# A kernel of attention, LSTM, three graph layers and a quantised product on one core: turned rows in the aggregation's bank, rounded passes in the first graph layer, products for the next scores behind the turned rows

## The reference, cut to what matters

```python
x = x + gat(layernorm(x), adj)        # 8 heads: masked softmax(q k / sqrt(32)) v, Wo, relu
x = x + lstm(layernorm(x))            # 256 steps over the nodes, 32 graphs at once
x = x + layers(layernorm(x), adj)     # below
x = x + fp8_product(layernorm(x))     # x and weight rounded to fp8, product, rescaled

def layers(x, adj):                   # L = 3
    for l in range(3):
        scores = (x @ w[l, :d])[:, :, None] + (x @ w[l, d:])[:, None, :] + b[l]
        scores = where(adj or own node, leaky(scores, 0.2), -inf)
        h = layernorm(x + softmax(scores) @ x) * g1[l] + beta1[l]
        ff = gelu(h @ W1[l] + b1[l]) @ W2[l] + b2[l]        # 256 -> 1024 -> 256
        x = layernorm(h + ff) * g2[l] + beta2[l]
    return x
```

## Time and profile before

| | us |
|---|---|
| median of 3 runs (2993.64 to 2996.24) | 2994.3 |
| profiled execution | 2992.49 |
| its span | 2990.7 |
| TensorE busy | 2683.2 (90%) |
| VectorE busy | 2052.4 (69%) |
| ScalarE busy | 1839.8 (62%) |
| GpSimd busy | 1620.6 (54%) |

### The profile page before, as it was taken

The page is one execution under the profiler, slowest core; times in us unless marked ns, Lnnn a source line. Parts: engine busy times, 40 slices in busy tenths (PEclk is TensorE's granted clock), DMA queues, the critical chain, the costliest instruction groups (busy, mean ns, idle before and its releaser), DMA issues. The chain is left out here.

```text
span 2990.7 us, 116485 instructions
## 1 busy us (share of the span) xinstructions
PE 2683.2 (90%) x44066; PEld 2435.4 (81%) x44224; DVE 2052.4 (69%) x6005; ACT 1839.8 (62%) x4930; POOL 1620.6 (54%) x2681
## 2 busy tenths in 40 slices
PE   6999999978888888859999999999999999999957
PEld 5777777767777777749999999899899999999956
DVE  6887888734444444446777776888888888888768
ACT  4666666644444444437777776777777677777734
POOL 6777777510000000037777765666666677788744
PEclk9999999989999999969999999999999999999979
DMA  3111111000000000020000011100000100000002
GB/s 92 40 35 35 35 41 38 13 10 13 12 13 12 13 13 13 13 76 25 26 23 25 26 44 31 27 7 9 9 7 9 45 9 9 9 7 9 8 25 91
DMA packets 110836, 74.59 MB, mean 25 GB/s; under 512 B 51504, under 2 KB 109360, under 8 KB 110512
## 3 DMA queue, kind: packets, MB, share of 16 engines
q1 hardware_dynamic: 96800, 61.03, 7.1%
q10 hardware_dynamic: 13968, 12.72, 1.4%
HBM read 51.68 MB, written 22.02 MB: 25 GB/s over the span
## 5 line engine op out<-in xcount | busy, mean ns | idle before, releaser
L1560 PE MATMUL g_H<-g_hT_upper,g_w_upper 128*128 128x256 f32 x1536 | 453.9, 295 | 0.0
L1560 PE MATMUL g_H<-g_hT_rest,g_w_upper 128*128 128x256 f32 x1536 | 436.0, 284 | 0.0
L1560 PE MATMUL g_H<-g_hT_upper,g_w_rest 128*128 128x256 f32 x1536 | 435.7, 284 | 0.0
L745 POOL COPY l_xt<-seq 128x64 f32 x256 | 60.6, 237 | 598.2 <-PE l_O L756 596.5
L1159 ACT ACTIVATE g_act_raw<-g_H,g_small 128x256 f32<-128x256 f32 x768 | 303.3, 469 | 22.2 <-PE g_H L1560 21.0
L329 ACT ACTIVATE a_probs<-a_S,a_nmax 128x256 f32<-128x256 f32 x512 | 236.7, 480 | 121.6 <-DVE a_nmax L422 88.9
L1051 POOL TENSOR_TENSOR g_h<-g_r,g_g_row 128x256 f32<-128x256 f32 x192 | 138.1, 741 | 294.7 <-DVE g_r L1360 294.0
L1560 PEld LDWEIGHTS g_H<-g_hT_rest,g_w_upper 128*128 128x128 f32 x1536 | 295.7, 193 | 2.5
L1560 PEld LDWEIGHTS g_H<-g_hT_upper,g_w_upper 128*128 128x128 f32 x1536 | 295.4, 192 | 2.7 <-DVE g_hT_rest L1308 0.2
L1587 PE MATMUL g_F<-g_w_upper,g_act_upper 128*128 128x256 f32 x1024 | 293.1, 286 | 4.5 <-DVE g_act_rest L1346 4.1
L1560 PEld LDWEIGHTS g_H<-g_hT_upper,g_w_rest 128*128 128x128 f32 x1536 | 295.8, 193 | 0.0
(11 more groups left out here) (222 smaller groups left out, 8658.8 us busy)
## 6 DMA issues: line engine op xcount, KB each, us to landing
gmask<-masks ACTq DMA_DIRECT2D x97, 128.0 KB, 2.0
x<-in_x_dram SPq DMA_DIRECT2D x32, 256.0 KB, 3.0
a_adj<-in_adj_dram SPq DMA_DIRECT2D x32, 256.0 KB, 2.7
hidden<-l_hs SPq DMA_DIRECT2D x512, 16.0 KB, 1.4
g_hs<-hidden SPq DMA_DIRECT2D x32, 256.0 KB, 2.7
out_dram<-q_res SPq DMA_DIRECT2D x32, 256.0 KB, 2.1
masks<-gmask SPq DMA_DIRECT2D x32, 128.0 KB, 1.7
g_w_raw<-in_L_gnn_W_dram SPq DMA_DIRECT2D x6, 512.0 KB, 4.0
```

The source lines that it names most:

```text
L745: pool.tensor_copy(xt[i][:, :, :], t.seq[:, :, s * 2 + i, :]).then_inc(xt_done, 1)
L1560: last = pe.matmul(hidden_bank[m // 2][:, m % 2 * N:(m % 2 + 1) * N], w[:, c, m * P:(m + 1) * P], x[:, c, :], start=(c == 0 and k == 0), s ...
```

## The change

Between attention and the end these parts are altered:

- graph layers: the rows are turned into `agg_bank`, the bias columns (`shift_bias`) into `turn_bank`; `turn_probs` no longer waits for `hT_done`, and a quarter of `up` goes ahead of it;
- first layer: `down` uses three rounded products for all banks but the first (`FIRST`), which stays float32 and goes between `aggregate` and the second half of `up`; `ON_ACT` gives ScalarE two of the roundings, and W2 is split there too;
- ScalarE: one bank's activations ahead of the slopes, `hT_out` between the dummy exponential and the exponentials; it makes the upper part of W1, which is split in halves;
- VectorE: `feed` ahead of `turned`, a bank's split between several steps, and `next_pair` behind `split_hT`;
- entry: LSTM outputs go by DMA into `t.nodes` directly, the first four with semaphores of their own; the start of the phase is reordered on all engines;
- attention: the first weights are waited for without Wo and biases; at the end `norm2` of the last two graphs is VectorE's, the one before the last is turned in `in_bank`, and weight scaling and bias split go ahead;
- last phase: its weight is loaded into `t.aw` during the third layer.

```diff
-                    sp.dma_start(w[:, :, :], src.rearrange("(c p) n -> p c n", p=P)).then_inc(weights_in, 16)
+                for w, src, done in ((wq, a["L0_gnn_Wq"], weights_in), (wk, a["L0_gnn_Wk"], weights_in),
+                                     (wv, a["L0_gnn_Wv"], weights_in), (wo, a["L0_gnn_Wo"], rows_in)):
...
+                split_bias()
                 spread_out(B - 1)
                 for b in range(B - 2, B):
                     rsqrt2(b)
-                    norm2(b)
-                split_bias()
...
+                    bank = in_bank if isinstance(b, int) and b == B - 2 else head_bank
+                    act.activation(t.seq[:, :, :, b], bank[:, :].rearrange("p (c n) -> p c n", c=KC),
...
-                rden_out(B - 1)
-                for b in range(B - 2, B):
-                    xn2T_out(b)
                 act.wait_ge(t.lstm_weights_in, LSTM_IN)
                 for w in (t.wx, t.wh):
                     act.activation(w[:, :, 0, :], w[:, :, 0, :], ACT.Copy, scale=0.5)
                     act.activation(w[:, :, 2:4, :], w[:, :, 2:4, :], ACT.Copy, scale=0.5)
+                rden_out(B - 1)
+                for b in range(B - 2, B):
+                    xn2T_out(b)
...
+                def norm2(b):
+
+                    dve.wait_ge(heads_ps, B)
+                    alone(dve, rstd2_done, b + 1, passed)
+                    for it in range(NT):
+                        last = dve.tensor_scalar(xn2[:, it, :], t.x[:, b, it, :], mv2[:, it, 0:1], rstd2[:, it, :],
+                                                 ALU.subtract, ALU.mult)
...
+                dve.wait_ge(weights_in, 3 * 16)
...
                 xnT_rest_out(0)
+                dve.wait_ge(rows_in, 5 * 16)
+                dve.memset(qscale[:, :], HD ** -0.5)
+                dve.tensor_scalar(bqs_col[:, :], bq_col[:, :], HD ** -0.5, None, ALU.mult).then_inc(bqs_done, 1)
+                moments1(1)
...
+                    if isinstance(b, int) and b == B - 2:
+                        pe.wait_ge(rden_done, B)
+                        turn(in_bank, xn2).then_inc(xn2T_ps, 1)
+                        return
...
+                    after(pe, xn2T_done, b if not isinstance(b, int) or b < B - 1 else B - 2)
...
+        ON_ACT = ((1, 3), (1, 3), (3,))
+        FIRST = (1, 0, 0)
...
+                def load_hidden(e, done):
+                    sp.dma_start(t.nodes[:, e, :, :], hidden[e].rearrange("(t p) d -> p t d", p=P)).then_inc(done, 16)
...
+                        load_hidden(4, hs_in)
+                        with sp.Fori(5, B) as e:
+                            sp.wait_ge(extra_x, e)
+                            load_hidden(e, hs_in)
+                sp.wait_ge(pair_done, 2 * (L - 1) * B)
+                sp.dma_start(t.aw[:, :, :], a["L1_ffn_weight"].rearrange("(c p) n -> p c n", p=P)).then_inc(t.ffn_weight_in, 16)
...
+                    for e in range(2):
                         enter(e)
                         rsqrt_extra(e)
+                    enter(2)
                     rsqrt1(*at)
+                    rsqrt_extra(2)
+                    enter(3)
+                    rsqrt_extra(3)
...
+                def w1_uppers(l, half):
+
+                    act.wait_ge(w1_in, (l + 1) * 16)
+                    act.wait_ge(cols_in, (l + 1) * COLS_IN)
+                    after(act, hidden_ps, l * B * NB)
+                    part = slice(half * FF // 2, (half + 1) * FF // 2)
+                    for c in range(KC):
+                        last = act.activation(w1_upper[:, c, part], w1_of(l)[:, c, part], ACT.Copy, scale=g1_col[:, c:c + 1])
...
+                    act.activation(hT_upper[:, :, :], agg_bank[:, :], ACT.Copy).then_inc(hT_upper_done, 1)
...
-                    for e in range(2):
-                        norm_extra(e, e)
+                    norm_extra(0, 0)
                     slope(*at)
+                    warm_up(*at)
                     attend(*at)
                     load_mask(*at)
+                    norm_extra(1, 1)
+                    w1_uppers(0, 0)
+                    w1_uppers(0, 1)
+                    slope(*soon)
+                    load_mask(*soon)
+                    norm1(*at)
+                    warm_up(*soon)
                     norm_extra(2, 2)
-                    norm1(*at)
                     hT_out(*at)
-                    slope(*soon)
                     attend(*soon)
-                    load_mask(*soon)
...
+                    crossing = ahead and now[0] < ahead[0]
+                    feed(*now, range(0, 1))
                     if soon:
                         slope(*soon)
                         load_mask(*soon)
-                    feed(*now, range(0, 2))
+                    feed(*now, range(1, 2))
...
                     feed(*now, range(2, NB))
+                    if crossing:
+                        w1_uppers(ahead[0], 0)
                     if ahead:
                         norm1(*ahead)
                     if soon:
-                        attend(*soon)
+                        warm_up(*soon)
                     if ahead:
                         hT_out(*ahead)
+                    if crossing:
+                        w1_uppers(ahead[0], 1)
+                    if soon:
+                        attend(*soon)
 
...
+                def split_w1(l, half):
+                    dve.wait_ge(w1_upper_done, 2 * l + half + 1)
+                    part = slice(half * FF // 2, (half + 1) * FF // 2)
                     for c in range(KC):
-                        last = dve.tensor_scalar(w1_upper[:, c, :], w1_of(l)[:, c, :], g1_col[:, c:c + 1], None, ALU.mult)
-                    last.then_inc(w1_upper_done, 1)
-                    dve.wait_ge(w1_upper_done, l + 1)
...
+                    moments_extra(0, 0)
                     dve.wait_ge(aw_first_in, 2 * 16)
-                    moments_extra(0, 0)
                     pair_entered(0)
                     as_neighbour(*at)
                     moments_extra(1, 1)
-                    split_w1(0)
                     largest(*at)
+                    reciprocals(*at)
+                    turned(*at)
                     pair_entered(1)
-                    reciprocals(*at)
                     as_neighbour(*soon)
-                    turned(*at)
+                    split_w1(0, 0)
+                    aggregated(*at)
                     moments_extra(2, 2)
-                    aggregated(*at)
+                    largest(*soon)
+                    split_w1(0, 1)
                     moments_extra(3, 3)
+                    shift_bias(0)
+                    split_hT(*at)
                     pair_entered(2)
-                    split_hT(*at)
-                    largest(*soon)
                     as_neighbour(*later)
-                    shift_bias(0)
...
+                    pairing = past and gone is None
+                    if behind:
+                        feed(*behind)
+                        stats2_of(*behind)
                     if ahead:
                         turned(*ahead)
                     if behind:
-                        feed(*behind)
+                        moments2(*behind)
+                    if first:
+                        split_w2(l, 0)
+                    if FIRST[l] == 0:
+                        split_act(l, b, range(0, 1))
                     if soon:
                         largest(*soon)
-                    if behind:
-                        stats2_of(*behind)
-                        moments2(*behind)
                     if ahead:
                         reciprocals(*ahead)
...
                         aggregated(*ahead)
-                    if in_parts(now[0]):
-                        split_act(*now, range(1, NB))
+                    split_act(l, b, range(1, 2))
+                    if first:
+                        split_w2(l, 1)
+                    split_act(l, b, range(2, 3))
                     if later and later[0] == 0:
                         pair_entered(later[1])
                     if later:
                         as_neighbour(*later)
+                    split_act(l, b, range(3, NB))
                     if crossing:
-                        split_w1(ahead[0])
+                        split_w1(ahead[0], 0)
                     if e is not None:
                         moments_extra(e, e)
                     if gone is not None:
                         if not (isinstance(gone, int) and gone == 0):
                             most_left(B + gone - 1, gone - 1)
                         moments_extra(B + gone, gone)
...
-                    if past and gone is None and not crossing:
-                        next_pair(*past)
                     if ahead:
                         split_hT(*ahead)
                     if crossing:
+                        split_w1(ahead[0], 1)
                         shift_bias(ahead[0])
-                        next_pair(*past)
+                    if pairing:
+                        next_pair(*past, 0)
```

(15 more changed lines are left out.)

160 lines of the change are left out of this document (71 added, 89 removed).

## The result

The changed kernel takes 2974.86 us (median of 4 runs, 2974.5 to 2975.25), the kernel before 2995.27 us on the same chip (4 runs, 2993.64 to 2998.04): ratio 0.9928, 95% interval 0.9914 to 0.9943. It is faster by 20 us where 42 were forecast. The profiled execution has a span of 2972.9 us (2990.7 before).

The account below looks back on a forecast made before the run. TensorE was taken to bound the first layer, and ScalarE's exponentials, delaying the turned rows, the others. Terms 36 + 1 - 31 - 19 - 1 - 11.6 - 9.5 - 3.5 - 2.2 = -42 from 2994.3: 2952 us, range 2907 to 2976.

Parts of the forecast that it names:

- The first layer: Rounded way down lengthens turns from 15.93 to 17.25 us on VectorE's chain: 27 x 1.32 = 36 us lost.
- Four holds: First layer: GpSimd's four scale and move products each lengthen one VectorE instruction, 2.0 us a turn together.
- Second and third layer: Exponentials leave the copy's way, turns fall to 15.0 us: 31 us gained in the second layer, 19 in the third.
- the chain's 15.05: Second and third layers: turned rows through ScalarE's copy and VectorE's rest to TensorE's start, 15.05 us into the turn.
- Is ScalarE free by then? 12.8: yes: Second and third layers: ScalarE is free at 12.8 us of the turn, before the copy is due at 13.7.
- Attention's start: First queries no longer wait for the splitting of weights after biases and Wo: 3.5 us gained.
- Attention's end: Earlier, faster projection, normalisation on VectorE and weight scalings moved ahead: 9.5 us gained, bounds 7 and 10.
- Start of the graph phase: Reordered entry, bias columns covering the wait for normalisation: first turn 11.6 us earlier, bounds 8 and 13.
- Last phase: Its weight is already loaded, so the wait of 2.30 us falls: 2.2 us gained.
- A: Rival: first layer bound by ScalarE or TensorE, holds hide, turns 15.85 us; total 2916, down to 2905; chance 0.27.
- C: Rival: GpSimd's residual products and entering addition also hold VectorE; turns up to 19.4 us, total 3010; chance 0.07.
- B: Rival: gains at the ends fail (late loads, low clock), third layer stays at 15.3 us; total 2974; chance 0.10.

Follow-up runs that it names:

- experiment 7: Changed kernel with TensorE's wait in each first-layer turn filled by twelve products whose result nobody reads: 2973.6 us, 0.9925.
- experiment 8: Changed kernel with ScalarE's exponentials ahead of the copy of the turned rows again in the second and third layers: 3017.1 us, 1.0067.
- after: The changed kernel itself, against the kernel before: 2974.86 us, ratio 0.9928.
- experiment 2: Changed kernel with GpSimd's scale and move ahead of the next graph's normalisation chain in the first layer: 2950.8 us, 0.9848.
- 12: Changed kernel with the edits of experiment 5 and experiment 11 together: 2943.6 us, 0.9827.
- experiment 5: Changed kernel; first layer: GpSimd's scale earlier, move at next turn's head, fourth bank's rounding on VectorE, entering graph's moments in its pause: 2940.1 us, 0.9811.
- experiment 11: Changed kernel with one unused GpSimd all-reduce of a zeroed tile behind its last LSTM copy: 2980.6 us, 0.9948.

## Why the prediction was wrong

**The first layer: the mechanism was right, the term 11.5 us too small.** The chain was followed correctly: third bank's activations done 10.15 us after the end of L1357 (10.0 forecast), then 7.26 us of VectorE's work up to the end of L1357 (5.3 + 2.0). Four holds of the forecast length, and the experiments show that taking them away takes 1.5 us off a turn. But a turn is 17.45, not 17.25, and over 27 graphs the 0.2 are 5.4 us. The activations ended 0.15 later than forecast, 0.09 of it because TensorE's first up-product starts 0.14 us after the rest and not 0.05, as the turned probabilities that stood there did in the second and third layer before; and the chain's 17.3 had been rounded down to 17.25. The other 6.8 us are a mechanism that the prediction had only at attention's end: the granted clock. TensorE's idle time was written down as 2.2 us a turn, and its effect on the clock was put at nothing without being asked for. In five places of the first layer the clock fell, and these turns were 1.3 to 1.45 longer; experiment 7 ties them to the wait. The first graph's splitting of W2 cost 0.2 where 1 was forecast, so that 11.5 of the 12.2 are seen in the table. One more term was wrong without binding: TensorE's own work in a turn is 17.45 - 1.88 = 15.57 us, not 15.0, so it waits 1.9 and not 2.3.

**Second and third layer: 8 us too much.** The 0.98 us of exponentials were the right cause: put back, they cost 42 us (experiment 8), and the wait at the head fell to the forecast's 0.2. The copy starts 13.7 us into the turn, as forecast, and takes, with the rest behind it, the 1.3 forecast. What was too small is the last step: TensorE starts 0.14 us after the rest in both layers, not 0.05, and the chain's 15.05 had been rounded to 15.0. TensorE's work between the waits is 14.97 and not 14.8, but with a wait of 0.2 left it does not set the turn. With 15.17 and 15.13 instead of 15.0, times 31 and 29, that is 5.3 and 3.8 us, where 4.5 and 3.8 are missing. "Is ScalarE free by then? 12.8: yes" held by luck: in the second layer ScalarE had waited 0.81 for GpSimd's normalisation and came straight from the dummy exponential to the copy, at 13.7 and no earlier. The fear that VectorE's queue binds in the third layer did not come true, by 0.19 us (its wait for the copy there).

**Attention's start: 3.5 us forecast, 0.6 seen at its end.** The first queries did begin 2.7 earlier (14.88 instead of 17.59 in the earlier trace rows), the first weighing of values only 1.3. The 12 products of the keys are the loss. Their durations (source view: smallest, median and largest ns), before and after:

```profile
L546 PE MATMUL a_Q<-a_xnT_upper,a_wk_upper x4: 274/280/389, 21.7 to 22.8; 128*128 128x256 f32 x4
```

```profile
L563 PE MATMUL a_Q<-a_xnT_upper,a_wk_upper x4: 415/415/580, 18.9 to 21.0; 128*128 128x256 f32 x4
```

Started 2.7 us earlier, they ran at little more than half the rate, which costs 12 x (0.213 - 0.117) = 1.2. In after the first record of the granted clock begins at 22.2 us, behind these products; in the kernel before it begins at 21.1, ahead of them. It is partly chance: in experiments 2 and 12 the same products began at 18.3 and 19.0 and were 0.117 apart, and there the first record begins at 17.8 and 17.9. The remaining 0.7 us are less than one trace can tell: in the twelve traces with this attention phase the last graph's weighing starts between 587.8 and 590.8.

**Attention's end: 7.9 of 9.5.** All steps are seen in TensorE's timeline, which answers to the earlier trace rows:

```profile
588.28 3.22 PE L635 MATMUL a_O<-a_probsT,a_v 128*32 128x256 f32 x32 [0.69 <-ACT a_probsT L338]
...
594.01 1.99 PE L651 MATMUL a_O<-a_wo,a_rden 128*128 128x256 f32 x8
600.72 1.12 PE L539 MATMUL a_O<-ident,a_xn 128*128 128x128 f32 x4 [4.72 <-DVE a_xn L473]
```

The projection is at full rate (1.99 for 3.75), as forecast. But the clock now fell during the weighing ahead of it, which took 3.22 us (1.94 before): 1.3 of the missing 1.6. TensorE in this stretch (window, length, busy time, granted clock, DMA):

```profile
588.28:591.50 3.22, 3.22 (x33) 0.58 0.00 0
```

This too is chance in part: in six of the twelve traces with this attention phase the weighing takes 3.2 to 3.6 us, in the other six 1.93.

**Start of the graph phase: 14.6 instead of 11.6.** The LSTM itself was 1.3 shorter (663.8 us from VectorE's first instruction to its last, 665.1 before), for no reason that I know. The other 1.7 lie at the bias columns, which the forecast had on the path at their old 6.83 us; they took 4.07 (timeline of TensorE):

```profile
1292.32 4.07 PE L1594 MATMUL g_T<-g_small,g_act_raw 128*128 128x1 f32 x32
```

The granted clock had been 0.50 for them and was 0.87 now (TensorE by windows, before and then after). They end 3.2 us earlier than forecast, 2.8 of it their own; behind them 3.9 us passed to the first turn where 2.4 were forecast, which takes back 1.5:

```profile
1316.70:1323.50 6.80, 6.80 (x34) 0.50 0.19 60
```

```profile
1292.32:1296.39 4.07, 4.07 (x34) 0.87 0.14 36
```

**Last phase: 0.5 of 2.2.** The weight was there, and VectorE's reduction ended 0.8 us into the phase instead of 3.2. The next step did not follow. GpSimd's all-reduce before and after (timelines):

```profile
2879.73 0.37 POOL L1688 PARTITION_ALL_REDUCE q_tops<-q_most  x1 [5.71 <-issue]
```

```profile
2862.35 0.37 POOL L1742 PARTITION_ALL_REDUCE q_tops<-q_most  x1 [5.63 <-issue]
```

It started 5.7 us after GpSimd's configuring instruction in both, whenever its input came: the 2.3 us for the load had lain beside these 5.7. "issue" as the releaser, with more than 5 us, was the sign to follow. The step of the last phase that failed is "the wait of 2.30 falls": it fell on VectorE, and I did not look who was late next. By the Trainium skill (GPSIMD Engine Reference, Instruction dispatch) the first call to a freshly loaded kernel pays some 6 us for code, with no instruction in the profile. The runs agree (5.6 to 6.0) and add that it is paid again at the next all-reduce, after other instructions.

**The whole.** The step of the prediction that failed most is the first layer's term, "27 x 1.32 = 36 us lost": these turns lost 47.6, 6.8 of it by falls of the clock, which the prediction had put at nothing without a reason. The next is TensorE's start 0.05 us behind the turned rows' rest, which was 0.14 in every layer, with a chain rounded down each time. Between the spans 17.8 us were gained of the 40.8 in the sum. Of the 23 missing, 11.5 are the first layer, 8.3 the other two, and 6.2 attention's two ends and the last phase; the graph phase's start gave back 3. Of the rivals, A and C did not come true, and of B's list (gains at the ends fail, the clock stays low) a good part did, beside the forecast's own loss. The forecast was right to count a loss in the first layer at all. What it didn't draw is the conclusion from its own sum: the rounded passes lose 44 us where they stand, and all the other edits are worth 66; and with GpSimd's `scale` and `move` placed otherwise the passes lose nothing.

## What to carry to other kernels

What work costs on VectorE depends on what GpSimd does beside it: ask beside what each added instruction will run, and try moving the neighbour before removing the work. When an edit moves one queue, write down what now keeps each neighbour in place, because an unwritten wait can be what kept two engines apart. And when a forecast says that TensorE will wait in every turn, add a price for its clock.

## What the runs showed of the hardware

**Short waits can cost the clock.** TensorE alone in two neighbouring stretches of the first layer (window, length, busy time, granted clock, DMA), in after and then with the wait filled:

```profile
1455.70:1459.10 3.40, 1.51 (x13) 1.00 0.00 0
1459.20:1462.60 3.40, 3.40 (x17) 0.50 0.00 0
```

```profile
1455.70:1459.10 3.40, 2.89 (x22) 1.00 0.00 0
1459.20:1462.60 3.40, 3.40 (x28) 1.00 0.05 12
```

In after TensorE had waited 1.89 us in the first stretch, and in the second the clock was at the lower of its two levels (1.2 of 2.4 GHz): 17 matmuls instead of 28. It happened five times in the layer, though the same wait was there in every turn; why in these turns and not in others stays open. Filled with products that nobody reads, the wait brought no fall, and neither did the waits of 1.2 us of experiment 5. The Trainium skill (TensorE: Matmul & The Clock Gate, Part 1) tells that "activity releases the throttle"; the runs agree, and show that the throttle can come back in the middle of a steady loop. At the very start the profile gives a clock of 1.00 while the products are 0.213 us apart, as in the stretch at 0.50 above; there the products are to be trusted.

**Each of GpSimd's 128x256 products of `scale` and `move` can hold one VectorE instruction** with inputs in SBUF, by some 0.55 us and little dependent on that instruction's size: 0.96 for 0.41, 0.97 for 0.43 on a cast (experiment 2), and 0.71 for 0.15 on one of two columns (experiment 5); on the rest of a bank it was 0.4 (1.11 and 1.09 for 0.69).

**An all-reduce over partitions costs GpSimd time before it and behind it:** 5.6 to 6.0 us before it each time. In experiment 11 the first addition of the graph phase came 8.6 us after GpSimd's configuring instruction (1270.86 to 1279.51), in after 3.4 us after the start of the phase, when its load had landed. The rows show how late the addition is; that it is a fetch of code is the Trainium skill's word, from the section named above, and its 6 us are for the first call alone.
